# Norm and gate at the ends of two scan layers: from phases over the whole image to a pipeline of tiles, with the inverse deviation taken once per pixel

## The chip, the cores and the metric

The kernel runs on one core of a Trainium2 chip. The metric is the time of one execution in microseconds (us) of device time; smaller is better. PE is the matrix engine (TensorE), PEld its weight loads, DVE is VectorE, ACT is ScalarE, POOL is GpSimd, SP issues nearly all DMAs. Every engine takes its instructions in program order and waits on semaphores. SBUF is the on-chip memory, PSUM the eight banks into which PE writes; POOL has no work on PSUM in this kernel.

## The reference, cut to what matters

Four layers run one after the other on an image x of 4 x 96 x 56 x 56: attention (layer 0), a scan layer with eight directions (layer 1), a local-window layer (layer 2) and a scan layer with four directions and a convolution block (layer 3). The change touches only what follows the scans in layers 1 and 3:

```
# layer 1, after the scans: y has 192 channels per pixel
mu  = y.mean(-1);  var = mean((y - mu)**2)            # over the 192 channels of a pixel
y   = (y - mu) / sqrt(var + 1e-5) * ln_w + ln_b
y   = y * silu(z)                                      # the gate
out = einsum('bhwd,od->bohw', y, w_out)                # 192 -> 96, then added to x

# layer 3, after the scans
u = ((y - mu) / sqrt(var + 1e-5) * ln_g + ln_b) * z    # the same norm and gate
t = relu(bn1(conv1x1(u, 192 -> 384)))
t = relu(bn2(depthwise3x3(t)))
t = conv1x1(t, 384 -> 96)
s = sigmoid(se2(relu(se1(t.mean over pixels))))
out = t + t * s                                        # then added to x
```

## The kernel before

The program is a list of stages. `chip.stage(pe, act, dve, pool, sp)` gives each engine its own instruction list, and a stage ends for all engines together: the next one starts behind a barrier. The order inside a stage is written by hand, with semaphores between the engines; no planner is at work.

Images are handled in pairs: 64 partitions hold channels of image 0, the other 64 those of image 1, so the 192 channels are three groups c of 64, and `yacc` is [128, 3 x 56 x w] (w is the row width, 64 in layer 1 and 56 in layer 3). A pixel tile is 8 rows of 56, T = 448 columns, and there are NT = 7 tiles. Each scan layer does, for each of the two pairs, a front, the scans, and a tail. So there are four tails: two of layer 1 (`tail1`, L1470) and two of layer 3 (`tail3`, L1567).

`TailNorm` (L1372) works through the tiles t. PE multiplies the three groups of `yacc` by `blk`, a block matrix that averages over 64 channels, and adds them up in PSUM: the mean, already copied to all 64 partitions of the image (L1392). DVE subtracts it (L1426). ACT squares (L1411), PE averages the squares in the same way (L1400), ACT takes the root of 128 x 448 (L1418), DVE takes the reciprocal of 128 x 448 (L1431) into `rstd`. Each pixel's value stands there 64 times. DVE does tile t's subtraction before tile t-1's reciprocal.

`Gate` (L1434) starts after the last reciprocal. For each tile and group DVE does y * lg * rstd (L1450) and (y + lb) * z (L1454). z comes from DRAM, two tiles deep (L1461).

In `tail1` PE multiplies each gated tile by `wo` for image 0 and image 1 (L1492, three matmuls each) into two PSUM banks, and DVE adds x (L1509). DVE's list has all 14 additions behind the whole gate, so PE, after two results, waits for the end of the gate.

In `tail3` the norm and the gate are a stage of their own (`tail3_norm`, L1574), and the convolution block is the next one (`tail3_block`, L1616). The block loads its weights and then takes image i = 0, 1. The first convolution makes 3 groups x 7 tiles (L1659), which ACT drains into a padded image `pad` (L1698). Only when all 21 are drained does the depthwise convolution begin. DVE does groups 0 and 1 as nine multiply-adds per tile (`taps`, L738 and L741); PE does group 2 as nine matmuls with diagonal matrices (L1671). ACT applies bn2 and relu (L1708, L1713), PE does the third convolution (L1647), ACT keeps it in `t3` with a running sum (L1689). After seven tiles the small dense layers on the mean follow (L1679, L1681), and DVE writes the result (L1740). Then the next image starts.

Of the kernel before, what the change touches and what calls it, by code (L numbers as in the profile page):

```python
# [7 lines left out]
F32 = mybir.dt.float32  # L8
# [9 lines left out]
C = 96  # L18
# [1353 lines left out]
class TailNorm:  # L1372


    def __init__(self, chip, sb, sems, K, yacc, w):
        self.PS, self.K, self.yacc, self.w = chip.PS, K, yacc, w
        self.rstd = sb("rstd", [128, L])
        self.sq = sb("sq", [128, 2, 3, T])
        self.sd = sb("sd", [128, 2, T])
        self.mean, self.centred, self.squared = sems("mean"), sems("centred"), sems("squared")  # L1380
        self.var, self.std, self.inverse = sems("var"), sems("std"), sems("inverse")
# [4 lines left out]
    def pe(self, e):  # L1386
        for t in range(NT + 1):
            if t < NT:
                if t >= 2:
                    e.wait_ge(self.centred, t - 1)  # L1390
                for c in range(3):
                    a = e.matmul(self.PS[:, t % 2, 0:T], self.K["blk"][:], self.y(c, t), start=(c == 0), stop=(c == 2))  # L1392
                a.then_inc(self.mean, 1)
            if t:
                u = t - 1
                e.wait_ge(self.squared, t)
                if u >= 2:
                    e.wait_ge(self.inverse, u - 1)
                for c in range(3):
                    a = e.matmul(self.PS[:, 2 + u % 2, 0:T], self.K["blk"][:], self.sq[:, u % 2, c, :],  # L1400
                                 start=(c == 0), stop=(c == 2))
                a.then_inc(self.var, 1)

    def act(self, e):
        for t in range(NT + 1):
            if t < NT:
                e.wait_ge(self.centred, t + 1)
                if t >= 2:
                    e.wait_ge(self.var, t - 1)
                for c in range(3):  # L1410
                    a = e.activation(rows8(self.sq[:, t % 2, c, :]), self.y(c, t), ACT.Square)  # L1411
                a.then_inc(self.squared, 1)
            if t:
                u = t - 1
                e.wait_ge(self.var, t)
                if u >= 2:
                    e.wait_ge(self.inverse, u - 1)
                e.activation(self.sd[:, u % 2, :], self.PS[:, 2 + u % 2, 0:T], ACT.Sqrt,  # L1418
                             bias=self.K["eps5"][:]).then_inc(self.std, 1)

    def dve(self, e):
        for t in range(NT + 1):
            if t < NT:
                e.wait_ge(self.mean, t + 1)
                for c in range(3):
                    a = e.tensor_tensor(self.y(c, t), self.y(c, t), rows8(self.PS[:, t % 2, 0:T]), ALU.subtract)  # L1426
                a.then_inc(self.centred, 1)
            if t:
                u = t - 1
                e.wait_ge(self.std, t)  # L1430
                e.reciprocal(self.rstd[:, u * T:u * T + T], self.sd[:, u % 2, :]).then_inc(self.inverse, 1)  # L1431
# [1052 lines left out]
```

## Time and profile before

| | us |
|---|---|
| median of 3 runs (18067.99 to 18101.3) | 18072.52 |
| the profiled execution's own time | 18087.81 |
| its span, first to last instruction | 18086.0 |
| the two tails of layer 1, from their first DMA to the next stage's | 6348.3 to 6462.7; 10602.7 to 10719.3 |
| the two tails of layer 3 | 14489.9 to 14880.6; 17693.6 to the end |

The profile is one execution. A row of the timeline view has the start, the duration, the engine, the source line, what is written from what, the number of instructions merged in the row, and in brackets how long the engine was idle before it and who ended that. A row of the window view has, for one stretch, each engine's busy time and instruction count, then the TensorE clock granted (1.00 is 2.4 GHz, 0.50 is 1.2 GHz), the DMA share and GB/s. A matmul of fp32 data counts as two records.

### The profile page before, as it was taken

The page shows a single profiled execution, that of the slowest core. Times are in us where ns is not written, and L with a number is a line of the kernel's source. Part 1 is how long each engine was busy: PE and PEld are TensorE (multiplying, and loading weights), DVE is VectorE, ACT ScalarE, POOL GpSimd, SP SyncE. Part 2 cuts the span into 40 slices and gives each one's busy share as a digit, 9 for nine tenths or more (in the row PEclk, how much of TensorE's full clock was granted, in tenths as well). Part 3 has the DMA queues.
Part 4 walks back from the last instruction along what each step waited for, and adds up shares of the span by engine and source line. Part 5 has one row for each costly group of instructions (what it writes and reads, how often), then busy time and mean ns, then how long its engine had stood idle before and what let it go on. Part 6 is the DMA issues. An engine that isn't in the chain of part 4 may idle for free. (4 is left out here: it accounts for less than half of the span.)

```text
span 18086.0 us, 184332 instructions
## 1 busy us (share of the span) xinstructions
PE 14292.3 (79%) x38972; PEld 5918.2 (33%) x38972; DVE 15507.5 (86%) x20601; ACT 11827.0 (65%) x24107; POOL 12383.2 (68%) x5929
## 2 busy tenths in 40 slices
PE   7998878888888868888888868767777767777776
PEld 2222233333333323333333325423333233333333
DVE  6666489999999979999999964489999958999996
ACT  3555556667777636767677734378888827888882
POOL 0000079999999939999999941179988806998881
PEclk9999899999999989999999977788888888888888
DMA  1000033333333323333333321122222212222220
GB/s 27 13 18 11 12 93 107 106 107 107 107 107 106 102 77 106 108 106 107 107 106 107 106 78 37 37 67 81 82 79 79 78 29 72 81 81 79 79 80 29
DMA packets 542714, 1404.62 MB, mean 78 GB/s; under 512 B 135503, under 2 KB 191863, under 8 KB 538599
## 3 DMA queue, kind: packets, MB, share of 16 engines
q1 hardware_dynamic: 541586, 1392.84, 27.0%
q14 instruction: 817, 6.69, 0.1%
q8 instruction: 311, 5.10, 0.1%
HBM read 1311.24 MB, written 58.30 MB: 76 GB/s over the span
## 5 line engine op out<-in xcount | busy, mean ns | idle before, releaser
L996 PE MATMUL PS<-Hc,ident 128*128 128x448 f32 x16128 | 7494.1, 598 | 1950.8 <-POOL Hc L1308 1596.6
L1300 POOL TENSOR_TENSOR Tr<-du,BC 128x1344 f32<-128x1344 f32 x2688 | 8161.1, 3036 | 60.7 <-DVE du L1179 60.5
L996 PEld LDWEIGHTS PS<-Hc,ident 128*128 128x128 f32 x16128 | 3106.2, 205 | 6212.5 <-POOL Hc L1308 2579.3
L1118 ACT ACTIVATE PS<-dl,A 128x448 f32<-128x448 f32 x5376 | 3403.3, 633 | 2049.9 <-DVE Hr L1226 1248.6
L1308 POOL TENSOR_TENSOR Hc<-Hr,BC 128x448 f32<-128x448 f32 (+1 forms) x2688 | 3892.6, 1448 | 1030.1 <-DVE Hr L1226 947.2
L1226 DVE TENSOR_TENSOR_SCAN PS<-PS,st,Tr 128x448 f32<-128x448 f32 x3072 | 3358.2, 1135 | 142.8 <-ACT st L1132 140.6
L1233 DVE TENSOR_TENSOR Hc<-PS,BC 128x448 f32<-128x448 f32 x4480 | 2564.0, 605 | 0.0
L1126 ACT ACTIVATE PS<-cs,lneps,A 128x448 f32<-128x448 f32 x2688 | 1941.0, 722 | 175.2 <-DVE PS L1226 171.6
L719 POOL MEMSET pad<- 128x348 f32 x6 | 2.3, 387 | 2800.6 <-POOLq L67 2800.6
L1209 DVE SCALAR_TENSOR_TENSOR PS<-PS,Tr 128x448 f32<-128x448 f32 x2688 | 1644.2, 612 | 225.0 <-ACT PS L1126 214.0
L1118 ACT ACTIVATE Ar<-dl,A 128x448 f32<-128x448 f32 x2688 | 1765.5, 657 | 0.0
L1226 DVE TENSOR_TENSOR_SCAN Hr<-PS,st,Tr 128x448 f32<-128x448 f32 x1536 | 1749.9, 1139 | 0.0
L1226 DVE TENSOR_TENSOR_SCAN Hr<-Ar,st,PS 128x448 f32<-128x448 f32 x1536 | 1742.3, 1134 | 0.0
L521 DVE TENSOR_REDUCE mx<-PS 128x1 f32<-128x448 f32 (+1 forms) x2100 | 1207.7, 618 | 569.8 <-PE PS L311 554.4
L470 ACT ACTIVATE Pr<-PS 128x896 f32<-128x896 f32 (+1 forms) x1092 | 953.7, 887 | 675.6 <-PE PS L374 672.0
L1226 DVE TENSOR_TENSOR_SCAN PS<-Ar,st,PS 128x448 f32<-128x448 f32 x768 | 877.7, 1143 | 0.0
L311 PE MATMUL PS<-K,Q 96*128 96x448 bf16 (+1 forms) x2100 | 799.5, 388 | 89.2 <-DVE mx L521 56.0
L1132 ACT ACTIVATE st<-PS 128x2 f32<-128x2 f32 (+1 forms) x2688 | 448.8, 167 | 637.8 <-DVE Hc L1233 622.4
L958 PE MATMUL PS<-dts,dw 12*128 12x448 f32 x1008 | 540.2, 616 | 347.0 <-ACT dl L1054 320.1
L1007 PE MATMUL PS<-yacc,ident 128*128 128x448 f32 (+15 forms) x1320 | 761.5, 685 | 36.6 <-ACT yacc L1109 36.2
L374 PE MATMUL PS<-Q,K 99*128 99x448 bf16 (+1 forms) x2100 | 750.7, 371 | 6.2 <-ACT Q L439 3.6
L953 PE MATMUL PS<-xs,xp 128*76 128x448 f32 x1008 | 472.5, 611 | 292.2 <-ACT xs L1031 291.9
(254 smaller groups left out, 16125.1 us busy)
## 6 DMA issues: line engine op xcount, KB each, us to landing
BC<-bcscratch SPq DMA_DIRECT2D x5376, 224.0 KB, 3.6
zscratch<-zst SPq DMA_DIRECT2D x84, 224.0 KB, 2.0
bcscratch<-rows SPq DMA_DIRECT2D x336, 56.0 KB, 2.9
z<-zscratch SPq DMA_DIRECT2D x28, 672.0 KB, 4.5
xg<-mid SPq DMA_DIRECT2D x12, 1176.0 KB, 8.3
xr<-mid SPq DMA_DIRECT2D x56, 168.0 KB, 2.6
rl<-rows SPq DMA_DIRECT2D x56, 168.0 KB, 3.5
Q<-part SPq DMA_DIRECT2D x72, 98.0 KB, 4.4
```

The source lines that it names most:

```text
L311: e.matmul(PS[0:qn, 5 + n % 2, 0:T], Q[s][0:96, q0:q0 + qn], KK[s][0:96, i * T:i * T + T], start=True, stop=True).then_inc(mx_mm, 1)
L470: e.activation(Pr[0:kn, n % NPR, 0:nt, :], PS[0:kn, 2 * (n % 2):2 * (n % 2) + nt, 0:T], ACT.Exp, scale=scale).then_inc(s_exp, 1)
L521: e.tensor_reduce(mx[0:qn, t, i:i + 1], PS[0:qn, 5 + n % 2, 0:T], AX.X, ALU.max).then_inc(mx_red, 1)
L996: e.matmul(PS[:, YB + c, 0:T], K["ident"][:], Hc[:, g % NHC, c, :], start=False, stop=(nn == 15)).then_inc(y_done, 1)
L1007: e.matmul(view(PS[:, YB + c, :], ro, rd), K["ident"][:], view(yacc, c * n + off, dims), start=(i == 0), stop=False)
L1118: e.activation(decay_at(u), dl[:, q % 2, c, :], ACT.Exp, scale=A[:, q // NT, c, nn:nn + 1]).then_inc(a_done, 1)
L1126: e.activation(PS[:, u % NW, 0:T], cs[:, q % 2, c, :], ACT.Tanh, scale=A2[:, q // NT, c, nn:nn + 1], bias=K["lneps"][:]).then_inc(w_done, 1)
L1209: e.scalar_tensor_tensor(out=p, in0=p, scalar=1.0, in1=Tr[:, g % NTR, c, :], op0=ALU.add, op1=ALU.mult).then_inc(t2_done, 1)
L1226: e.tensor_tensor_scan(state_at(g, c), decay_at(u), PS[:, u % NW, 0:T] if ratio else Tr[:, g % NTR, c, :], 0.0 if q % NT == 0 else st[:, n ...
L1233: e.tensor_tensor(Hc[:, g % NHC, c, :], state_at(g, c), BC[:, g % NBS, 1, :], ALU.mult).then_inc(h_done, 1)
L1300: e.tensor_tensor(Tr[:, g % NTR], du[:, q % 2], b, ALU.mult).then_inc(t_done, 1)
L1308: e.tensor_tensor(Hc[:, g % NHC, ON_DVE:3], Hr[:, g % NH], c_, ALU.mult).then_inc(hp_done, 1)
```

## The change

1. `TailNorm` and `Gate` become one class, `NormGate`, whose steps are methods for one tile, and each engine's list goes by rounds r: tile r is centred and squared, tile r-1 is normalised and scaled, tile r-2 is shifted and gated, tile r-3 goes into the layer's next matmuls.
2. The mean: DVE adds the three groups (two additions), PE does one matmul instead of three.
3. The deviation: POOL adds the three squares (two additions); PE then multiplies with the sums as the stationary operand and two columns of `blk` as the moving one, so that pixels stand on partitions: 112 x 8 values per tile for both images. ACT's root and DVE's reciprocal are of 112 x 8. ACT copies them to 112 x 512 (`wide`), and four matmuls with the identity spread them to 128 x 448 in PSUM.
4. The scaling stays on DVE (L1474 of the new kernel), the shift by lb goes to ACT, the product with z to POOL.
5. In layer 1 the output matmuls use four PSUM banks and the additions of x stand in the rounds.
6. In layer 3 norm, gate and block are one stage, in rounds over 14 steps k (7 tiles x 2 images): the first convolution of step r-3, the depthwise one of step r-5, the third of step r-6. The depthwise group 2 is PE's only in the 8 steps of `PE_TAPS`; in the other 6 DVE does it too. `t3` holds both images, and the result is written and stored in halves.

```diff
+    def dve_sum(self, e, t):
+        s = rows8(self.ysum[:, t % 2, :])
+        ...
+        e.tensor_tensor(s, self.y(0, t), self.y(1, t), ALU.add).then_inc(self.summed, 1)
+        e.wait_ge(self.summed, 2 * t + 1)
+        e.tensor_tensor(s, s, self.y(2, t), ALU.add).then_inc(self.summed, 1)
+    def pe_mean(self, e, t):
+        e.wait_ge(self.summed, 2 * t + 2)
+        ...
+        e.matmul(self.PS[:, 5, 0:T], self.K["blk"][:], self.ysum[:, t % 2, :], start=True, stop=True).then_inc(self.mean_mm, 1)
+    def pool_sum(self, e, t):
+        s = self.sqsum[:, t % 2, :]
+        e.wait_ge(self.squared, t + 1)
+        ...
+        e.tensor_tensor(s, self.sq[:, t % 2, 0, :], self.sq[:, t % 2, 1, :], ALU.add).then_inc(self.sq_summed, 1)
+        e.wait_ge(self.sq_summed, 2 * t + 1)
+        e.tensor_tensor(s, s, self.sq[:, t % 2, 2, :], ALU.add).then_inc(self.sq_summed, 1)
+    def pe_var(self, e, t):
+        ...
+        for q in range(4):
+            a = e.matmul(self.PS[0:112, 6, 2 * q:2 * q + 2], self.sqsum[:, t % 2, 112 * q:112 * q + 112],
+                         self.K["blk"][:, 0:128:64], start=True, stop=True)
+    def act_root(self, e, t):
+        ...
+        e.activation(self.sd[:, t % 2, :], self.PS[0:112, 6, 0:8], ACT.Sqrt, bias=self.K["eps5"][0:112, :]).then_inc(self.rooted, 1)
-                e.reciprocal(self.rstd[:, u * T:u * T + T], self.sd[:, u % 2, :]).then_inc(self.inverse, 1)
+        e.reciprocal(self.rs[:, t % 2, :], self.sd[:, t % 2, :]).then_inc(self.inverse, 1)
+    def act_widen(self, e, t):
+        ...
+        e.activation(self.wide[:, t % 2].rearrange("p q (i c) -> p (q i) c", i=2),
+                     self.rs[:, t % 2, :].unsqueeze(2).broadcast_to([112, 8, 64]), ACT.Copy).then_inc(self.widened, 1)
+    def pe_spread(self, e, t):
+        e.wait_ge(self.widened, t + 1)
+        ...
+        for q in range(4):
+            a = e.matmul(self.PS[:, 7, 112 * q:112 * q + 112], self.wide[:, t % 2, q, :], self.K["ident"][0:112, 0:112],
+                         start=True, stop=True)
+    def dve_scale(self, e, t):
+        ...
+            a = e.scalar_tensor_tensor(out=y, in0=y, scalar=self.lg[:, c:c + 1], in1=rows8(self.PS[:, 7, 0:T]), op0=ALU.mult, op1=ALU.mult)
+    def act_shift(self, e, t):
+        ...
+            a = e.activation(self.y(c, t), self.y(c, t), ACT.Identity, bias=self.lb[:, c:c + 1])
+    def pool_gate(self, e, t):
+        e.wait_ge(self.shifted, t + 1)
+        e.wait_ge(self.z_ld[t % 2], 16 * (t // 2 + 1))
+        for c in range(3):
+            a = e.tensor_tensor(self.y(c, t), self.y(c, t), rows8(self.z[:, t % 2, c, :]), ALU.mult)
...
+PE_TAPS = (0, 1, 2, 4, 6, 8, 11, 13)
...
         def pe(e):
...
+            e.wait_ge(w_ld, 112)
+            for r in range(NK + 6):
+                if r < NT:
+                    norm.pe_mean(e, r)
+                if 0 <= r - 1 < NT:
+                    norm.pe_var(e, r - 1)
+                if 0 <= r - 3 < NK:
+                    expand(r - 3, 0)
+                if 0 <= r - 1 < NT:
+                    norm.pe_spread(e, r - 1)
+                if 0 <= r - 3 < NK:
+                    expand(r - 3, 1)
+                    expand(r - 3, 2)
+                if r - 5 in PE_TAPS:
+                    tap(r - 5)
...
+                if 0 <= r - 6 < NK:
+                    reduce_(r - 6)
```

DVE in layer 3, the first tail, from the gate into the block before (`rstd` inverse deviations, `w_484` the weights of the first convolution, `pad` its padded output, `acc` the depthwise sums):

```order
 L1450 SCALAR_TENSOR_TENSOR yacc<-yacc,lg,rstd 128x448
 L1454 SCALAR_TENSOR_TENSOR yacc<-yacc,lb,z 128x448
 L39 UNCONDITIONAL_BRANCH
 L42 UNCONDITIONAL_BRANCH
 L1724 MEMSET w_484 128x2304
 L738 TENSOR_SCALAR acc<-pad,cw 128x448
 L741 SCALAR_TENSOR_TENSOR acc<-pad,cw,acc 128x448 x8
```

The same place now, rounds 5 and 6 (`rs` inverse deviations by pixel):

```order
 L1410 TENSOR_TENSOR yacc<-yacc,PS 128x448 x3
 L1451 RECIPROCAL rs<-sd 112x8
 L738 TENSOR_SCALAR acc<-pad,cw 128x448
 L741 SCALAR_TENSOR_TENSOR acc<-pad,cw,acc 128x448 x8
 L1474 SCALAR_TENSOR_TENSOR yacc<-yacc,lg,PS 128x448 x3
 L738 TENSOR_SCALAR acc<-pad,cw 128x448
 L741 SCALAR_TENSOR_TENSOR acc<-pad,cw,acc 128x448 x8
 L1410 TENSOR_TENSOR yacc<-yacc,PS 128x448 x3
```

The depthwise sums of the first steps stand between the centring and the scaling of tiles 5 and 6, with no stage border in front.

PE in the first tail of layer 1, from the norm to the output matmuls before (`sq` squares, `wo` output weights):

```order
-L1392 MATMUL PS<-yacc,blk 128x448 x3
-L1400 MATMUL PS<-sq,blk 128x448 x6
-L1492 MATMUL PS<-yacc,wo 96x448 x42
```

And one round of it now (`ysum` sum of the groups, `sqsum` sum of the squares, `wide` the copied inverses):

```order
+L1405 MATMUL PS<-ysum,blk 128x448
+L1436 MATMUL PS<-blk,sqsum 112x2 x4
+L1525 MATMUL PS<-yacc,wo 96x448 x3
+L1465 MATMUL PS<-ident,wide 128x112 x4
+L1525 MATMUL PS<-yacc,wo 96x448 x3
```

The output matmuls of tile r-3 stand on both sides of the spread of tile r-1, and the mean of the next tile stands behind the second three.

## Rows read from the trace of the kernel before

**Rows 1.** The page: busy time, share of the span, instructions.
```profile
PE 14292.3 (79%) x38972; PEld 5918.2 (33%) x38972; DVE 15507.5 (86%) x20601; ACT 11827.0 (65%) x24107; POOL 12383.2 (68%) x5929
```
**Rows 2.** Windows: PE, PEld, DVE, ACT, POOL busy, clock, DMA; the tails by stage.
```profile
6348.30:6462.70 114.40, 72.77 (x168) 31.75 (x168) 67.70 (x85) 15.70 (x29) 0.01 (x1) 0.85 0.29 86
10602.70:10719.30 116.60, 72.88 (x168) 31.54 (x168) 67.70 (x85) 15.70 (x29) 0.00 (x0) 0.82 0.29 84
14489.90:14574.00 84.10, 37.88 (x84) 17.06 (x84) 60.02 (x80) 16.18 (x31) 0.00 (x0) 0.76 0.19 58
14574.00:14880.60 306.60, 244.27 (x596) 115.31 (x596) 173.34 (x259) 71.72 (x117) 16.56 (x30) 0.89 0.07 19
17693.60:17778.40 84.80, 39.02 (x84) 17.77 (x84) 60.03 (x80) 16.18 (x31) 0.01 (x1) 0.74 0.19 57
17778.40:18086.00 307.60, 244.82 (x596) 115.17 (x596) 173.33 (x259) 71.70 (x117) 16.55 (x29) 0.89 0.07 19
```
**Rows 3.** Timeline, first tail of layer 1, the norm.
```profile
6352.47 1.68 DVE L1426 TENSOR_TENSOR yacc<-yacc,PS 128x448 f32<-128x448 f32 x3 [3.43 <-PE PS L1392]
...
6371.02 1.51 ACT L1411 ACTIVATE sq<-yacc 128x448 f32<-128x448 f32 x3 [4.55 <-DVE yacc L1426]
6372.44 0.61 ACT L1418 ACTIVATE sd<-PS,eps 128x448 f32<-128x448 f32 x1
6372.58 2.52 PE L1400 MATMUL PS<-sq,blk 128*128 128x448 f32 x6 [1.80 <-ACT sq L1411]
6373.08 2.95 DVE L1431 RECIPROCAL rstd<-sd 128x448 f32<-128x448 f32 x1 [2.09 <-ACT sd L1418]
```
**Rows 4.** Timeline, the same tail, gate and output.
```profile
6400.31 0.68 DVE L1450 SCALAR_TENSOR_TENSOR yacc<-yacc,lg,rstd 128x448 f32<-128x448 f32 x1
...
6436.55 0.62 DVE L1509 TENSOR_TENSOR yo<-PS,xr 96x448 f32<-96x448 f32 x1 [1.63 <-PE PS L1492]
...
6459.10 0.62 DVE L1509 TENSOR_TENSOR yo<-PS,xr 96x448 f32<-96x448 f32 x1 [1.63 <-PE PS L1492]
```
**Rows 5.** Groups by form: count, busy us, mean ns, idle before.
```profile
L1431 DVE RECIPROCAL rstd<-sd 128x448 f32<-128x448 f32 x28 | 82.7, 2952 | 62.5 <-ACT sd L1418 62.5
L1308 POOL TENSOR_TENSOR Hc<-Hr,BC 128x448 f32<-128x448 f32 x1792 | 2026.7, 1131 | 507.1 <-DVE Hr L1226 436.9
L1698 ACT ACTIVATE pad<-PS,bn1o 128x448 f32<-128x448 f32 x84 | 61.0, 726 | 222.2 <-PE PS L1659 222.2
```
**Rows 6.** Timeline, a 112 x 112 fp32 matmul of layer 2, six of them.
```profile
10909.86 1.44 PE L1929 MATMUL PS<-dg,E 112*84 112x112 f32 x12
```
**Rows 7.** Timeline, layer 3's block: weights' arrival, DVE's waits, one group.
```profile
14582.19 18.13 PE L1659 MATMUL PS<-yacc,w 128*128 128x448 f32 x40 [42.15 <-DMA w<-in_c1w]
...
14633.51 0.45 DVE L738 TENSOR_SCALAR acc<-pad,cw 128x448 f32<-128x448 f32 x1 [56.93 <-ACT pad L1698]
...
14639.65 0.45 DVE L738 TENSOR_SCALAR acc<-pad,cw 128x448 f32<-128x448 f32 x1
...
14776.79 0.45 DVE L738 TENSOR_SCALAR acc<-pad,cw 128x448 f32<-128x448 f32 x1 [45.16 <-ACT pad L1698]
```
**Rows 8.** Timeline, end of the program: last depthwise sum to store.
```profile
18061.97 5.73 DVE L741 SCALAR_TENSOR_TENSOR acc<-pad,cw,acc 128x448 f32<-128x448 f32 x8
...
18079.14 0.32 SPq L1758 DMA_DIRECT2D out<-xr  x1
```
**Rows 9.** PE's third convolution after waits of two lengths.
```profile
17900.65 2.50 PE L1647 MATMUL PS<-cv,w 128*96 128x448 f32 x6 [1.30 <-ACT cv L1713]
...
17912.91 3.97 PE L1647 MATMUL PS<-cv,w 128*96 128x448 f32 x6 [3.00 <-ACT cv L1713]
```
**Rows 10.** DVE and POOL together, in a front.
```profile
2290.34 5.90 DVE L741 SCALAR_TENSOR_TENSOR acc<-pad,cw,acc 128x448 f32<-128x448 f32 x8
2290.74 0.71 POOL L851 COPY xc<-xc 128x448 f32<-128x448 f32 x1 [65.09 <-ACT xc L819]
```

**Rows 11.** The page: DMA issues, KB each, us to landing.
```profile
z<-zscratch SPq DMA_DIRECT2D x28, 672.0 KB, 4.5
```

More of the change, by code:

```diff
@@ L1404, in act @@
[L1404 to L1419, printed above, removed]
@@ L1477, in tail1 @@
         wo_zero, w_ld, l_ld = sems("wo_zero"), sems("w_ld"), sems("l_ld")
-        norm = TailNorm(chip, sb, sems, K, yacc, w)
-        gate = Gate(sb, sems, norm, zd, pair, lg, lb)
+        norm = NormGate(chip, sb, sems, K, yacc, w, zd, pair, lg, lb)
         out_mm, added = sems("out_mm"), sems("added")
@@ new lines, in pe, with drain, relu @@
+            squeeze(1)
+            excite(1)
+        def act(e):
+            def drain(k, c):
+                t = k % NT
+                u = place[k, c]
+                if u == 0:
+                    e.wait_ge(pad_zero, 1)
+                    e.wait_ge(folds[0].step, 5)
+                if k >= NT:
+                    e.wait_ge(tapped, 9 * tap_groups(min(k - NT + 1, NT - 1)))
+                    e.wait_ge(relued, min(k - NT + 2, NT))
+                e.wait_ge(full, u + 1)
+                e.activation(pad[:, c, 1 + 8 * t:9 + 8 * t, 1:57], rows8(PS[:, u % 4, 0:T]), ACT.Relu,
+                             scale=bn1[:, 0, c:c + 1], bias=bn1[:, 1, c:c + 1]).then_inc(drained, 1)
+            def relu(k):
+                v = k % 2
+                if k == 0:
+                    e.wait_ge(folds[1].step, 5)
+                if k >= 2:
+                    e.wait_ge(red_mm, k - 1)
+                if k in PE_TAPS:
+                    u = place[k, "tap"]
@@ new lines, in act @@
+            e.wait_ge(l_ld, 96)
+            for f in folds:
+                f.act(e)
+            e.wait_ge(w_ld, 112)
+            for r in range(NK + 7):
+                if 0 <= r - 2 < NT:
+                    norm.act_shift(e, r - 2)
+                if r < NT:
+                    norm.act_square(e, r)
+                if 0 <= r - 1 < NT:
+                    norm.act_root(e, r - 1)
+                    norm.act_widen(e, r - 1)
+                if r == NT + 8:
+                    squeeze(0)
+                if 0 <= r - 7 < NK:
+                    keep(r - 7)
+                if 0 <= r - 6 < NK:
+                    relu(r - 6)
+                if r == NT + 8:
+                    excite(0)
+                for c in range(3):
+                    if 0 <= r - 3 < NK:
+                        drain(r - 3, c)
@@ L1748, in sp @@
         def sp(e):
+            for t, k in ((lg, "l3lg"), (lb, "l3lb"), (b1, "c1b"), (b2, "c2b"), (folds[0].t, "bn1"), (folds[1].t, "bn2")):
+                e.dma_start(t[:], D[k]).then_inc(l_ld, 16)
+            for t in range(2):
+                norm.load(e, t)
             for t, k in ((cw, "c2w"), (w3, "c3w"), (c3b, "c3b"), (s1w, "s1w"), (s1b, "s1b"), (s2w, "s2w"), (s2b, "s2b")):
```

476 lines of the change are left out of this document (261 added, 215 removed).

## The prediction

> **What bounds the kernel now.** I read the page first: DVE is busy 86% of the span, PE 79% [rows 1]. That average is set by the scans, where the change does nothing, so the next view is the windows over the four tails. They last 114.4, 116.6, 84.1 + 306.6 and 84.8 + 307.6 us, 1014.1 in all, 5.6% of the span. DVE is busy 602 us of that, PE 712, POOL 33 [rows 2]: nobody is full, the engines take turns. The timeline says how. In the norm one tile takes 6.58 us, a closed loop: reciprocal 2.95, the next subtraction 1.61, squares 1.51, root 0.61, reciprocal again [rows 3]. The gate is DVE's alone, 84 instructions at two per 1.4 us, about 29 us per tail. In layer 1 PE then makes the outputs, one per 2.25 us [rows 4]. In the block DVE stands still 56.9 and 45.2 us while PE makes the first convolution of an image, then works without a gap at 6.13 us per group of nine [rows 7].
>
> **Durations of the new steps.** Known from rows: three subtractions 1.65, three squares 1.51, three matmuls 2.25 (0.75 each) with 0.2 more until the last is done [rows 3, 4]. Two additions of SBUF tiles on DVE: like the subtraction, 0.55 each, 1.25 with the wait between them. Scaling: three of 0.68, less their overlap, 1.9 [rows 4]. Shift on ACT: like the squares, 1.6. POOL: 1.13 per product or sum [rows 5], so 2.3 for the two sums and 3.4 for the gate. Copy to 112 x 512: a square of 448 is 0.5, so 0.65. The trace does not show the small steps. A root of 112 x 8 lies between 0.1 and the 0.61 of the large one, a reciprocal of 8 between 8/448 of 2.95, that is 0.05, and 0.6 of any DVE instruction; I take 0.25 for each, nearer to the lower ends because work by element is gone. Four small matmuls: the nearest row is six of 112 x 112 in 1.44, 0.24 each [rows 6], so 1.0 and 1.2 until done; upper end 0.4 each, if weight loads of 128 columns don't hide. Hand-over between engines: 0.05 (square ends 6372.53, PE starts 6372.58) [rows 3].
>
> The Trainium skill weighs against item 3 here: "GPSIMD Engine Reference", section "Key points", says that POOL shares its SBUF interfaces with VectorE and that instructions with two SBUF inputs contend. The trace agrees in size: eight multiply-adds of DVE took 5.90 beside one 0.71 us copy of POOL [rows 10], and 5.73 alone [rows 8].
> From these rows alone: 0.17 us per 0.71 of POOL, so 0.3 per POOL instruction of 1.13. About 12 of them per layer-3 tail fall beside depthwise sums, 4 us; in layer 1 the pairs of additions meet some, 2 us.
>
> **Tail of layer 1.** Fill: the first subtraction ends 5.8 us after the start as now [rows 3]. Then tile 0: squares 1.5, sums 2.3, small matmuls 1.2, root and reciprocal 0.5 (with the table load that stands there now too, and ACT still squaring tile 1, some 2.5 more), copy 0.65, spread 1.2, scale 1.9, shift 1.6: 19 us. POOL must sum tile 2 first, whose squares are behind the shift: 1.5 + 2.3; gate 3.4. The first output matmul starts at about 29.
> Then the rounds. The loop in one is: subtraction 1.65, squares 1.5, root 0.25, reciprocal 0.25, copy 0.65, spread 1.2, three output matmuls 2.25 that stand in front of the next mean, mean 0.95, eight hand-overs 0.4: 9.1, with a small lag 9.3. DVE's own work is 7 per round, POOL's 5.7, PE's 7.2, so the loop binds. Three rounds bring outputs 0 to 5: 57. The next has no mean: 8.3, so 65.5. Six outputs are left, 13.5 plus 2 for the last gate: 81. Addition 0.6, store and barrier 3.0 (6459.72 to 6462.7 now [rows 4]): 85. With 2 for contention 87. Gains 27.4 and 29.6, together 57.
>
> **Tail of layer 3.** DVE's work grows: 34 groups instead of 28, since 6 of 14 steps keep all three, 34 x 6.13 = 208.4. What goes is the standing still.
> Start: PE waits for seven small loads that now stand behind six others and two z loads in SP's queue: 15 issues of about half a us and a landing. Now the block needs 8.2 us from its start to its weights [rows 7], the new stage about 11 to 13. The wait holds the first mean, so everything. Rounds 1 to 4 then run as in layer 1, with PE's 6.75 of first convolution (3 x 2.25) in rounds 3 and 4: first depthwise group at about 64. Rounds 5 and 6 are PE's: small norm work with its ends 3.1, first convolution 6.75, depthwise on PE 9 x 0.75 = 6.75, third 2.25, 19 together, against 12.3 of groups and 5 of norm on DVE. So at about 99 four groups are done. From there DVE has no wait: 30 x 6.13 = 183.9, last scaling 1.9, image 0's result 3.9: 289. PE needs 6.75 to 15.75 per round there, against 12.3 and 18.4 of DVE, and by the two-step lead it stays ahead. ACT's drains, 0.73 each [rows 5], lie beside that. From the last group to the last store 11.4 as now (18067.7 to 18079.14) [rows 8]: 300. The store now takes 6.9 to the end of the span [rows 2, 8]; half the size, 4.5. Sum 304.5, with 4 for contention 308. Gains 390.7 - 308 = 82.7 and 392.4 - 308 = 84.4: 167.
>
> **Sum.** 57 + 167 = 224. Against the profiled execution 18087.8 that makes 17864; against the median of the runs, 15.3 lower, 17849. I forecast 17849. The scans, fronts and the other layers have the same instructions. Lower end: no contention (12 less) and small steps at the low ends (8 rounds x 0.5 x 4, 16 less): 17821. Upper end of the same mechanism: small matmuls at 0.4 instead of 0.24 put 1.3 on each of the 8 rounds' loops twice over: 10 per tail, 42 in all: 17891.
>
> **Rivals.**
> A: PE paces the block. If reductions, drains and depthwise matmuls wait for each other within a round (bank u waits for the drain of u-4, which waits behind ACT's relu, which waits for DVE), the rounds with PE groups cost PE's 15.75 and not the mean of PE and DVE: 8 x 3.5 = 28 more per tail, 56 in all, or as much from a slow clock in half of them. For it: the first convolution of step k+2 and DVE's groups of step k hang on the same ACT queue. Against: in rounds 5 to 18 DVE has some 222 of work, PE 173 (81 + 54 + 29 + 9). Time 17905.
> B: z arrives late. SP issues z of tile t+2 behind stores that wait for additions. A load lands 4.5 us after its issue [rows 11]. If POOL waits for a whole landing in 5 rounds of both layer-1 tails, that is 45 us: 17894. Layer 3 has no stores in between. The lead of about one round, 9 us, speaks against it.
> C: slower than before. PE's clock: after a wait of 1.30 us six records took 2.50, after 3.00 us 3.97 [rows 9], near 1.2 GHz. The new rounds have waits inside them in place of one long one between phases. If PE ran at 1.2 GHz through all four tails, it would need in a layer-3 tail 247 large matmuls x 1.5 + 56 small x 0.5 = 398, plus fill and end 52: 450; a layer-1 tail, with spread, output and mean doubled in the loop, 125. Sum 1150 against 1014: 136 slower, 18209. DVE's 254 (208 of groups, 7 x 5.1 of norm, some 10 of the rest) hides PE's 199 (247 x 0.75 + 56 x 0.24) up to a factor of 1.3; the gain is gone at about 1.7 (199 x 1.7 + 52 is the 390 of now), a mean clock of 0.6. Against: the tails are at 0.74 to 0.89 now, with waits [rows 2].
> The Trainium skill has the rule for this: "TensorE: Matmul & The Clock Gate", section "HAM oscillation", tells of a kernel that waits between its bursts and starts every burst slow. By rows 9 that holds for waits of 3 us; the rounds' longest is about that in the fill only.
> D: better than the forecast, because the fill (64 us in layer 3) is shorter and contention nil: 17810.
>
> **How the numbers follow.** Forecast 0.62; A 0.20; B 0.07; C 0.04; D 0.05; 0.02 that it gains nothing for a reason not seen. The range 17815 to 17930 leaves out D's far end, C and the worst of A: about 0.15. The measurement tells apart 0.2%, 36 us. Faster by more than that: all of forecast, A, B and D, less a little, 0.94; within 0.02; slower 0.04.
>
> **What would show it.** Right: no 128 x 448 reciprocal, and reciprocals of 112 x 8 near 0.2; rounds of 9 to 9.5 us in layer 1; the block's DVE from the fourth group on without idle time until image 1 ends; DVE's waits of 56.9 and 45.2 us gone, in their place waits of a few us between the norm's steps until the first group; stages of 87 and 308. Wrong: DVE idle before its groups behind ACT (A), POOL idle behind the z load (B), a granted clock under 0.65 in the tails (C), multiply-adds of DVE well over 0.69 in more than a few places. The whole would be wrong if the other stages change their length by more than 10 us.

## The result, and the profile after

The changed kernel took 17862.85 us in the median of four runs (17858.43 to 17872.52), the kernel before 18080.18 beside it (median of four runs, the three behind the 18072.52 above among them): ratio 0.9879, 95% interval 0.9862 to 0.9896. A second set of runs on another occasion gave 17867.53 and 0.9884 (0.9871 to 0.9898). The forecast was 17849.

The page first: busy time, share, instructions, as in [rows 1].

```profile
span 17859.1 us, 184766 instructions
PE 14124.2 (79%) x38924; PEld 5866.3 (33%) x38924; DVE 15511.5 (87%) x20685; ACT 11881.7 (67%) x24219; POOL 12534.2 (70%) x6033
```

Over the whole span DVE is as busy as before (15507.5 then), and the span is 226.9 us shorter. That total hides two opposite moves, which the windows below show against [rows 2]: in a layer-1 tail DVE's busy time fell from 67.7 to 44.1 and 44.6 us, since half of the gate and nearly all of the reciprocal left it, and in a layer-3 tail it rose from 233.4 to 259.0 and 259.6, since it took six more groups. In layer 3 the gain is therefore waiting that went. In layer 1 the tails lost 30 us each, and DVE's work shrank by 23 to 24 at the same time; no run changed the order and left the work where it was, so the two are not told apart there. The windows over the four tails, columns as in [rows 2]; in layer 3 one window stands where there were two:

```profile
6341.50:6425.80 84.30, 62.11 (x210) 34.16 (x210) 44.11 (x78) 29.94 (x57) 39.34 (x35) 0.78 0.39 117
10562.90:10648.90 86.00, 61.24 (x210) 33.47 (x210) 44.64 (x78) 29.93 (x57) 40.08 (x35) 0.81 0.38 114
14417.50:14731.90 314.40, 222.95 (x614) 111.78 (x614) 259.04 (x388) 99.27 (x176) 50.30 (x46) 0.85 0.12 34
17546.00:17859.10 313.10, 224.29 (x614) 112.45 (x614) 259.61 (x388) 99.47 (x176) 50.68 (x46) 0.84 0.12 34
```

The tails last 797.8 us against 1014.1: 216.3 less, where 224 was forecast. Layer 1 gave 60.7 (57 forecast), layer 3 155.6 (167 forecast). The other 10.6 of the span's difference lie outside the tails (18086.0 - 1014.1 = 17071.9 before, 17061.3 after). The eleven executions of the experiments have 17039.6 to 17075.9 there, with the same instructions in all of them, so this is scatter, and the windows of the tails measure the change better than the whole time does.

One round of layer 1 in the timeline (start, length, engine and line; in brackets the idle time before and what ended it), to hold against the loop of [rows 3]:

```profile
6379.19 1.67 DVE L1410 TENSOR_TENSOR yacc<-yacc,PS 128x448 f32<-128x448 f32 x3
6380.89 1.51 ACT L1418 ACTIVATE sq<-yacc 128x448 f32<-128x448 f32 x3 [2.34 <-DVE yacc L1410]
6382.30 0.25 ACT L1444 ACTIVATE sd<-PS,eps 112x8 f32<-112x8 f32 x1
6382.58 0.20 DVE L1451 RECIPROCAL rs<-sd 112x8 f32<-112x8 f32 x1 [1.73 <-ACT sd L1444]
6382.82 0.63 ACT L1457 ACTIVATE wide<-rs 112x512 f32<-112x512 f32 x1 [0.27 <-DVE rs L1451]
6383.50 1.81 PE L1465 MATMUL PS<-ident,wide 112*128 112x112 f32 x8 [2.17 <-ACT wide L1457]
...
6385.35 1.86 DVE L1474 SCALAR_TENSOR_TENSOR yacc<-yacc,lg,PS 128x448 f32<-128x448 f32 x3 [2.06 <-PE PS L1465]
...
6389.36 1.15 DVE L1410 TENSOR_TENSOR yacc<-yacc,PS 128x448 f32<-128x448 f32 x2
```

From subtraction to subtraction 10.17 us. The reciprocal's 2.95 us have become 0.20, and from its start to the scale's it is 2.77 us still: widening and spreading stand there now.

The same view of VectorE in the first layer-3 tail: the weights' wait, the first groups, the last group and the end.

```profile
14428.77 0.63 DVE L1397 TENSOR_TENSOR ysum<-yacc 128x448 f32<-128x448 f32 x1 [4.90 <-DMA s2b<-in_s2b]
...
14481.97 0.20 DVE L1451 RECIPROCAL rs<-sd 112x8 f32<-112x8 f32 x1 [1.73 <-ACT sd L1444]
14482.09 1.15 DVE L738 TENSOR_SCALAR acc<-pad,cw 128x448 f32<-128x448 f32 x1
14483.27 8.74 DVE L741 SCALAR_TENSOR_TENSOR acc<-pad,cw,acc 128x448 f32<-128x448 f32 x8
...
14494.18 5.73 DVE L741 SCALAR_TENSOR_TENSOR acc<-pad,cw,acc 128x448 f32<-128x448 f32 x8
...
14504.54 8.75 DVE L741 SCALAR_TENSOR_TENSOR acc<-pad,cw,acc 128x448 f32<-128x448 f32 x8
...
14515.46 7.99 DVE L741 SCALAR_TENSOR_TENSOR acc<-pad,cw,acc 128x448 f32<-128x448 f32 x8
...
14523.48 0.40 DVE L738 TENSOR_SCALAR acc<-pad,cw 128x448 f32<-128x448 f32 x1
...
14531.82 7.98 DVE L741 SCALAR_TENSOR_TENSOR acc<-pad,cw,acc 128x448 f32<-128x448 f32 x8
...
14709.46 5.73 DVE L741 SCALAR_TENSOR_TENSOR acc<-pad,cw,acc 128x448 f32<-128x448 f32 x8
14720.85 0.16 DVE L1842 TENSOR_REDUCE sm<-sums 96x1 f32<-96x7 f32 x1 [5.67 <-ACT t L1795]
```

The waits of 56.9 and 45.2 us of [rows 7] are gone. From the fourth group's end (14523.4) to the last group's (14715.2) VectorE has no idle time. Groups of eight multiply-adds take 5.73 us, as in [rows 8], but four take 7.98 to 8.75. GpSimd in that stretch:

```profile
14481.86 1.12 POOL L1426 TENSOR_TENSOR sqsum<-sq 128x448 f32<-128x448 f32 x1 [4.79 <-ACT sq L1418]
14483.07 1.16 POOL L1428 TENSOR_TENSOR sqsum<-sqsum,sq 128x448 f32<-128x448 f32 x1
14484.19 4.46 POOL L1488 TENSOR_TENSOR yacc<-yacc,z 128x448 f32<-128x448 f32 x3
...
14516.96 4.57 POOL L1488 TENSOR_TENSOR yacc<-yacc,z 128x448 f32<-128x448 f32 x3 [7.04 <-ACT yacc L1481]
14533.32 4.56 POOL L1488 TENSOR_TENSOR yacc<-yacc,z 128x448 f32<-128x448 f32 x3 [11.79 <-ACT yacc L1481]
```

Each long group lies beside a row of three products like these (the one beside the group of 14504.54 starts at 14505.46 and takes 4.46), and these rows are long too: in layer 1, where VectorE is idle or reads PSUM meanwhile, three products take 3.32 us.

### The profile page after: what moved, and what is told of

It reads as the page before. It is cut to its first block and busy times, and to the rows that moved or that the text cites. A ratio compares the mean times of both kernels' runs of the same rounds, so it can differ in the third digit from the quotient of the medians.

```text
span 17859.1 us, 184766 instructions
## 1 busy us (share of the span) xinstructions
PE 14124.2 (79%) x38924; PEld 5866.3 (33%) x38924; DVE 15511.5 (87%) x20685; ACT 11881.7 (67%) x24219; POOL 12534.2 (70%) x6033
## 5 line engine op out<-in xcount | busy, mean ns | idle before, releaser
L1233 DVE TENSOR_TENSOR Hc<-PS,BC 128x448 f32<-128x448 f32 x4480 | 2563.5, 604 | 0.0
L741 DVE SCALAR_TENSOR_TENSOR acc<-pad,cw,acc 128x448 f32<-128x448 f32 x992 | 701.1, 707 | 35.5
```

The source lines that it names most:

```text
L741: e.scalar_tensor_tensor(out=o, in0=x, scalar=cw[:, c, k:k + 1], in1=o, op0=ALU.mult, op1=ALU.add).then_inc(done, 1)
L1233: e.tensor_tensor(Hc[:, g % NHC, c, :], state_at(g, c), BC[:, g % NBS, 1, :], ALU.mult).then_inc(h_done, 1)
```

## The experiments

For each kernel the four tails are read from its trace, from the tail's first load of its parameters to the next stage's first load (or the end of the span); "median" and ratio are of its runs against the kernel before in the same session. The rows marked * are one execution each.

| kernel | layer 1 | layer 3 | sum | median us | ratio |
|---|---|---|---|---|---|
| changed | 84.3, 86.0 | 314.4, 313.1 | 797.8 | 17862.85 | 0.9879 |
| only_tail1 | 84.4, 86.4 | 389.6, 388.9 | 949.3 | 18002.82 | 0.9961 |
| full_recip | 100.8, 103.1 | 323.1, 321.6 | 848.6 | 17903.49 | 0.9904 |
| recip_psum * | 93.0, 92.8 | 316.8, 318.0 | 820.6 | 17881.15 | |
| small_gate | 85.4, 86.9 | 305.4, 310.7 | 788.4 | 17844.74 | 0.9871 |
| dve_gate * | 86.7, 84.7 | 313.5, 312.8 | 797.7 | 17847.54 | |
| late_wait | 84.7, 84.5 | 310.5, 311.5 | 791.2 | 17842.92 | 0.9873 |
| taps11 | 86.5, 86.2 | 295.3, 297.5 | 765.5 | 17818.80 | 0.9863 |
| taps14 * | 84.2, 84.7 | 304.6, 304.8 | 778.3 | 17856.17 | |
| late_taps12 * | 86.8, 85.9 | 288.1, 288.4 | 749.2 | 17790.90 | |
| changed, again | 86.3, 85.9 | 313.6, 314.4 | 800.2 | 17867.53 | 0.9884 |
| final | 84.3, 86.4 | 287.3, 287.2 | 745.2 | 17803.68 | 0.9851 |

Intervals of the ratios are 0.0013 to 0.0017 to either side. A layer-1 tail that two kernels share differs by up to 2.6 us, and the layer-3 tail that only_tail1 shares with the kernel before by up to 3.5, so a difference of 1 to 3 us in one tail is not evidence by itself.

**Half the change: only_tail1.** `tail1` and `NormGate` as changed; `tail3`'s norm, gate and block stages as before.

> The first layer's tails as changed, the second layer's norm stage and convolution stage as before. If the gain is what each stage's own window shows, the two layer-1 tails take 84 and 86 us (114.4 and 116.6 before), the layer-3 stages stay at 84 + 307 us each, and the time is about 61 us below before: ratio 0.9966, some 18019 us. The rival is that part of the layer-3 gain, or of the 10 us that the changed kernel is shorter by outside its tails, comes from elsewhere in the program (the scan of layer 1, which starts earlier or later beside other transfers): then layer 3 of this kernel is shorter too, and the time is below 18010 us.

Measured: 84.4 and 86.4 us in layer 1, 389.6 and 388.9 in layer 3, 0.9961 (0.9946 to 0.9976). The gain is local, stage by stage. The median, 18002.8, was 16 us under the expectation, which alone would have pointed to the rival; the windows show layer 3 shorter by 1 to 3.5 us only and the rest (17049.2 us) inside its scatter.

**The reciprocal of 128x448 back: full_recip.**

```diff
-        for q in range(4):
-            a = e.matmul(self.PS[0:112, 6, 2 * q:2 * q + 2], self.sqsum[:, t % 2, 112 * q:112 * q + 112], ...)
+        a = e.matmul(self.PS[:, 6, 0:T], self.K["blk"][:], self.sqsum[:, t % 2, :], start=True, stop=True)
...
-            a = e.scalar_tensor_tensor(out=y, ..., in1=rows8(self.PS[:, 7, 0:T]), ...)
+            a = e.scalar_tensor_tensor(out=y, ..., in1=rows8(self.rs[:, t % 2, :]), ...)
```

Root and reciprocal are of 128x448 here, and the widening and the spread are left out.

> The pipeline and the one stage of layer 3 are kept, but the variance goes through one 128x448 product with the averaging matrix, and root and reciprocal are taken of 128x448, with no widening and no spreading products. Theory: what a round waits for is a chain, and the chain from the small reciprocal (0.20) over the widening (0.63) and the spreading products to the scale's start is already 2.8 to 3.0 us, as long as a reciprocal of 128x448 alone (2.95 in the kernel before). So the layer-1 tails grow only by the root (0.25 to about 0.5 us a round, 8 rounds): 86 and 88 us. In layer 3 VectorE sets the pace from the first depthwise group on, and three reciprocals lie behind it, 3 x 2.75 = 8 us, with 2 us before it: 324 us a tail. Sum about 24 us above the changed kernel, 17887 us, ratio 0.9892. The rival: the small reciprocal is where the gain comes from, as VectorE's busy time has it: 28 x 2.75 = 77 us more, 17940 us, ratio 0.992.

Measured: 50.8 us more in the tails (848.6 - 797.8), between the two theories (24 and 77). Layer 3 came near the expected 10 (8.7 and 8.5 us more), by luck in part, as the next run shows; layer 1 did not: 16.5 and 17.1 more in place of 2. VectorE's groups of that tail (count, busy us, mean ns, idle before), first with the large reciprocal, then of the changed kernel:

```profile
L1471 DVE SCALAR_TENSOR_TENSOR yacc<-yacc,lg,rs 128x448 f32<-128x448 f32 x21 | 20.9, 1045 | 0.1
L1448 DVE RECIPROCAL rs<-sd 128x448 f32<-128x448 f32 x7 | 20.7, 2953 | 15.8 <-ACT sd L1441 15.8
```

```profile
L1474 DVE SCALAR_TENSOR_TENSOR yacc<-yacc,lg,PS 128x448 f32<-128x448 f32 x21 | 13.0, 676 | 14.6 <-PE PS L1465 14.6
L1451 DVE RECIPROCAL rs<-sd 112x8 f32<-112x8 f32 x7 | 1.4, 203 | 13.3 <-ACT sd L1444 13.3
```

The scale, the same arithmetic on the same shape, went from 676 to 1045 ns, 7.9 us a tail. What had changed in this instruction is where its second operand lies: SBUF in place of PSUM.

**The operand moved: recip_psum.** Against full_recip:

```diff
-        e.reciprocal(self.rs[:, t % 2, :], self.sd[:, t % 2, :])
+        e.reciprocal(self.PS[:, 7, 0:T], self.sd[:, t % 2, :])
```

The scale reads the same bank. One bank stands in place of two buffers, so the reciprocal also waits for the scale of the tile before, which stands ahead of it in VectorE's list in any case.

> As the kernel with the reciprocal of 128x448, but VectorE writes the reciprocal into a PSUM bank and the scale reads it there, not in SBUF. In that kernel the scale's 21 instructions took 20.9 us of a layer-1 tail, the longest 1552 ns, against 13.0 us and 672 to 681 ns where they read PSUM. Theory: an instruction of VectorE with both tensors in SBUF is stretched while GpSimd's product runs, one with a tensor in PSUM is not. So the scale goes back to 675 ns and 13.0 us, and the layer-1 tails shrink by nearly 8 us each, 93 and 95 us; in layer 3 (20.0 us now) by 5 to 7 us of the 323 and 322. The rival: the scale is slower because GpSimd's product or the matmuls read the same tensor y at that time; then it stays near 1 us an instruction and the tails keep 101 and 103 us.

Measured: 93.0, 92.8, 316.8 and 318.0 us. One line of code, all its instructions in the trace (least, median and longest ns), with the operand in SBUF and in PSUM:

```profile
L1471 DVE SCALAR_TENSOR_TENSOR yacc<-yacc,lg,rs x84: 671/682/1552, 6344.5 to 17710.8; 128x448 f32<-128x448 f32 x84
```

```profile
L1471 DVE SCALAR_TENSOR_TENSOR yacc<-yacc,lg,PS x84: 664/676/681, 6346.8 to 17676.8; 128x448 f32<-128x448 f32 x84
```

The operand in PSUM takes 848.6 - 820.6 = 28 us off the tails. The rival, that GpSimd's product or the matmuls read the same `yacc` at that time, is refuted: they still do. So 28 of full_recip's 51 us are contention that came with the operand in SBUF, and the narrow root and reciprocal with all that belongs to them are worth the other 820.6 - 797.8 = 23, of one execution and so known to a few us. By VectorE's busy time it would have been 77.

The chain had given 24, but in other places, so that the agreement is luck: it put 2 us on a layer-1 tail and 10 on a layer-3 tail, and the differences are 8.7 and 6.8 in layer 1 and 2.4 and 4.9 in layer 3. In the first layer-1 tail GpSimd's waits for z behind the last rounds are 4.84 and 3.96 us here, against 1.16 and 2.82 in the changed kernel: late z, the prediction's rival B, is part of the 8.7. In layer 3 GpSimd's two sums of squares and the start of its product now fall beside the reciprocal and no longer beside a group: two groups take 7.23 us in place of 8.75, and their first products 0.38 in place of 1.15, so 4.6 us of contention go as the long reciprocals come.

**GpSimd's product cut: small_gate.** In layer 3, tiles 3 to 6, `y, z = y[:, 0:1, :], z[:, 0:1, :]` ahead of the product, so that 56 of 448 columns are gated and the others are left out.

> In layer 3 POOL's product with z for tiles 3 to 6 covers only the first 56 of 448 columns; the other columns of these tiles are left without the gate. All else as changed. Theory: the four depthwise groups that VectorE runs beside these products are longer for that: 8.74, 8.75, 7.99 and 7.98 against 5.73 us, of which the product has 2.26 us each (7.99 - 5.73, the groups that no sum of squares lies beside). They come down to 6.5, 6.5, 5.7 and 5.7 us, and each layer-3 tail is 9 us shorter: 305 and 304 us, 18 us in all. The rival: these groups are longer for another reason (their place behind a wait, the matmuls' reads, ScalarE's), they keep 8 to 8.7 us, and the tails stay at 314 us.

VectorE in the second of the loaded rounds, against 8.75 and 7.99 above:

```profile
14503.20 6.49 DVE L741 SCALAR_TENSOR_TENSOR acc<-pad,cw,acc 128x448 f32<-128x448 f32 x8
...
14511.86 5.73 DVE L741 SCALAR_TENSOR_TENSOR acc<-pad,cw,acc 128x448 f32<-128x448 f32 x8
14518.54 0.20 DVE L1451 RECIPROCAL rs<-sd 112x8 f32<-112x8 f32 x1 [0.95 <-ACT sd L1444]
```

The mechanism and its size are shown: 2.26 us a group, 9 us in the first layer-3 tail. The first of these groups keeps 0.76 us over 5.73; the second sum of squares still runs beside its start. The second tail gained 2.4 us only, not 9: its first group came 1.6 us later than in the changed kernel (64.4 us into the stage, not 62.8), and the reciprocal of tile 6 was waited for.

```profile
17620.29 6.92 PE L1708 MATMUL PS<-yacc,w 128*128 128x448 f32 x12
...
17627.06 6.93 PE L1719 MATMUL PS<-pad,diag 128*128 128x448 f32 x18
...
17637.27 0.20 DVE L1451 RECIPROCAL rs<-sd 112x8 f32<-112x8 f32 x1 [4.03 <-ACT sd L1444]
```

The same twelve records took 4.69 us in the first tail. There the granted clock was 1.00 (14502.8 to 14508.3); here it was 0.50 (17618.4 to 17624.0). So TensorE came 2.2 us later to its 18 depthwise records, the variance products stand behind these, and VectorE's next group stands behind the reciprocal. When VectorE's groups shrink, TensorE's order is the next thing late.

**The same product on VectorE: dve_gate.** Tiles 3 to 6 in layer 3: `e.scalar_tensor_tensor(out=y, in0=y, scalar=lb, in1=z, op0=ALU.add, op1=ALU.mult)`, without ScalarE's shift.

> In layer 3 the gate of tiles 3 to 6 goes from ScalarE (shift) and GpSimd (product) to VectorE, as (y + beta) * z in one instruction for each channel block, in the round in which GpSimd had it. Theory: the product beside a group costs VectorE 2.26 us (7.99 against 5.73 us); four of them, 9.0 us a tail. On VectorE itself a tile costs 3 instructions of 0.62 us as the scale does (1.86 us), 7.4 us for four. So the two nearly cancel: the tails are 313 and 312 us, 1 to 2 us shorter. The rival: it is the engine that counts and not the neighbour, all that VectorE gets is added: 314 + 7 = 321 us. A second rival is that the reciprocal of tile 6 is then waited for (it was, by 0.95 and 4.03 us, where the product had been cut), and half of what is won goes there.

Measured: 313.5 and 312.8 us. All its groups take 5.73 us again, and the gates took what that won:

```profile
14494.69 3.45 DVE L1497 SCALAR_TENSOR_TENSOR yacc<-yacc,lb,z 128x448 f32<-128x448 f32 x3
...
14498.54 5.73 DVE L741 SCALAR_TENSOR_TENSOR acc<-pad,cw,acc 128x448 f32<-128x448 f32 x8
...
14513.93 1.86 DVE L1497 SCALAR_TENSOR_TENSOR yacc<-yacc,lb,z 128x448 f32<-128x448 f32 x3
```

Of the four gates two took 3.45 us, those beside the sums of squares, and two 1.86: 10.6 us, not 7.4. The reciprocal of tile 6 was waited for by 1.63 us besides. Giving GpSimd the product costs VectorE 2.26 us a tile, and doing it itself costs 1.86 or more: in this place the offload is worth nothing.

**The weights' wait: late_wait.**

```diff
-            e.wait_ge(w_ld, 112)            # ahead of all rounds, on PE, ACT and DVE
             for r in range(NK + 5):
+                if r == 5:                  # DVE; PE r == 6, ACT r == 7, POOL r == 2
+                    e.wait_ge(w_ld, 112)
```

> In the one stage of layer 3, the wait for the seven weights' transfers is taken at the weights' first use (VectorE and GpSimd in the rounds before the first depthwise group, TensorE and ScalarE behind it) and not ahead of the norm. Theory: VectorE waits there 4.9 us for the last of them, 11.2 us from the stage's start, and all that follows up to the first depthwise group is a chain, so the first group starts about 4 us earlier (60.5 us from the start, not 64.5) and each layer-3 tail is 4 us shorter: 310 and 309 us. The rival: the wait only moves; z of the first tiles, the affine weights or the first 1x1 weights (which stand behind the seven transfers in the same queue) or the zeroing of the padded buffer come last in its place, and less than 1 us is left.

```profile
14405.98 0.63 DVE L1397 TENSOR_TENSOR ysum<-yacc 128x448 f32<-128x448 f32 x1 [1.27 <-PEq L67]
...
14466.09 1.15 DVE L738 TENSOR_SCALAR acc<-pad,cw 128x448 f32<-128x448 f32 x1
```

The first depthwise instruction starts 60.2 us into the stage (64.6 in the changed kernel), in the second tail 60.3 (62.8). The tails are 3.9 and 1.6 us shorter, where the theory had 4. The 1.6 is within the scatter; what shows the effect in the second tail is its first group, 2.5 us earlier.

**The balance of the two engines: taps11, taps14.** `PE_TAPS` with 11 and with 14 tiles in place of 8.

> As changed, but TensorE takes the third channel block's depthwise products of 11 tiles of 14 (0, 1, 2, 3, 4, 5, 7, 8, 10, 11, 13) and not of 8: VectorE has 31 groups left of 34. Theory: VectorE alone sets the pace of the block in the changed kernel too (no idle time between the fourth group and the last), so each group less is worth 6.13 us: 3 x 6.13 = 18.4 us a layer-3 tail, 296 and 295 us, less what TensorE's longer rounds give back (18 records of 6.93 us for each such tile; 2 to 4 us where two of them follow each other): 297 to 300 us, some 30 to 35 us below the changed kernel in all. The rival: TensorE already paces part of the block (rival A of the prediction), and the tails stay at 310 us or above.

> As changed, but TensorE takes the third channel block of all 14 tiles; VectorE has 28 groups, six fewer. If VectorE were the only bound, the layer-3 tails would come to 314 - 6 x 6.13 = 277 us. Theory: TensorE becomes it. A tile costs it 6.93 (expansion) + 6.93 (depthwise) + 2.42 (reduction) = 16.3 us at the full clock, 14 of them 228 us, with the norm's products (7 x about 4.5) and a first expansion that starts some 33 us into the stage, and 15 us behind the last reduction: 305 to 310 us, no more than 10 us below the changed kernel's 314, and above the tails with 11 tiles.

Measured: 295.3 and 297.5 us with 11, 304.6 and 304.8 with 14. Three groups less on VectorE (18.4 us by 6.13) gave 19.1 and 15.6: with 8 tiles VectorE alone paces the block. With 14, VectorE's waits in the first tail (total, times, longest) have a new head:

```profile
DVE acc L738 <- ACT pad L1771: 25.3, 5, 15.2
DVE rs L1451 <- ACT sd L1444: 11.0, 6, 2.4
```

The groups wait 25.3 us for ScalarE's drains (L1771), which stand behind TensorE's expansions. So the best number lies between 8 and 14.

**Both: late_taps12, and timed again as final.**

> The late wait for the weights and 12 tiles of 14 with the third channel block on TensorE (all but 7 and 10). Theory: the two are independent. Four groups less are 4 x 6.13 = 24.5 us a tail, the late wait 4 and 2 us as measured alone; TensorE has 12 x 16.3 + 2 x 9.35 = 214 us of the block against VectorE's 30 x 6.13 = 184 us, so it now waits for TensorE in places: 288 to 295 us a tail. The rival: TensorE is the bound already at 12 tiles, and this is no shorter than 11 tiles would be with the late wait (293 us), or longer.

> The changed kernel itself once more, for comparison on the same chip: 17863 us within 10, its tails 84, 86, 314 and 313 us within 2. Its tails are the same from one execution to the next to 1 or 2 us, while the rest of the program (the front ends and scans, 17039 to 17076 us in the kernels run so far, none of which touches it) scatters by more.

> The late wait and 12 tiles with the third channel block on TensorE, timed: tails of 86, 86, 288 and 288 us as in its first execution, 797.6 - 748 = 49 us below the changed kernel's; with the rest of the program its own scatter, 17800 to 17820 us, ratio 0.985 to 0.986. The rival: the 17791 us of the one execution were a stroke of luck in the rest, and the layer-3 tails' gain is given back elsewhere: 17840 us or more.

Late_taps12's tails were 288.1 and 288.4 us, final's (the same kernel) 287.3 and 287.2. That is 25 to 27 us under the changed kernel's tails, where four groups (24.5) and the late wait's 3.9 and 1.6 make 28.4 and 26.1: within 3 us the two edits add up. 12 tiles without the late wait were not tried, nor 13. Final's windows of layer 3, columns as in [rows 2]:

```profile
14414.50:14701.80 287.30, 241.00 (x686) 124.17 (x686) 233.50 (x352) 98.45 (x176) 50.26 (x46) 0.90 0.13 37
17514.50:17801.70 287.20, 240.86 (x686) 124.43 (x686) 233.53 (x352) 98.46 (x176) 50.28 (x46) 0.89 0.13 37
```

TensorE and VectorE are now about equally busy, at 241 and 234 of 287 us. Final took 17803.68 us (17796.06 to 17818.02), 0.9851 (0.9837 to 0.9864) of before, against 0.9884 for the changed kernel in the same session: 0.36% faster than it (17803.68 against 17867.53), and the fastest version here. The 17791 of the one execution was low by its rest (17039.6 against 17056.5).

## Why the prediction was right, and where it was off

- **The bound, "the engines take turns".** Right as far as the windows show it: all four tails together keep DVE busy for 607 us, against 602 before, and lost 216 us. only_tail1 shows 60 of it to be layer 1's own. How much of that is overlap, and how much the work that left DVE, is open.
- **The small steps, 0.25 us each for root and reciprocal of 112 x 8.** Measured 0.25 and 0.20 (medians of 28).
- **Layer 1: first output matmul at 29 us, rounds of 9.3, tail 87.** Measured 26.9, 9.8, 10.2 and 8.5 (starts of L1410 at 6369.36, 6379.19, 6389.36, 6397.89), 84.3 and 86.0. The loop was the right thing to sum. The 29 was not what its own terms make: 19, 1.5 + 2.3 and 3.4 are 26.2, close to what came, and the surplus of nearly 3 us is about what the first tail came out under 87. The sign "rounds of 9 to 9.5" held for the mean only. The round of 10.2 is one in which TensorE was slow: granted clock 0.66 (6383.5 to 6388.5), against 1.00 in the round of 8.5 (6393.7 to 6397.0).
- **Layer 3: weights at 11 to 13, first group at 64, four groups done at 99, last group at 289.** Measured 11.2, 64.6, 105.9, 297.6. The order of events is right and nearly all of the excess arises between the first group and the sixth.
- **The step that was off: contention, "about 12 of them per layer-3 tail, 4 us".** It is 11.9 us in the first tail: the four groups are longer by 3.01, 3.02, 2.26 and 2.25 us, and two first products by 0.70 each (1.15 against 0.45). The count was near (four gates and two pairs of sums, 16 instructions); the price was not: 0.75 us for each of a gate's three instructions (2.26 / 3), where the estimate had 0.3. It came from [rows 10], a copy of 0.71 us, which reads one tensor; GpSimd's products read two. The prediction's "the trace agrees in size" has nothing to agree with, since the page that it cites states no size. And its own sign of being wrong, multiply-adds well over 0.69 us in more than a few places, came true in four of 34 groups a tail. 8 us more on 308 makes 316, and 314.4 and 313.1 were measured: all other terms together were 2 to 3 us too high.

  A better price stood in the trace before, overlooked. An instruction of VectorE with two SBUF tensors took 0.95 us beside a product of GpSimd (11422.02 to 11423.15), and 0.47 without one:

```profile
11422.54 0.95 DVE L2162 SCALAR_TENSOR_TENSOR E<-R,E 112x315 f32<-112x315 f32 x1
...
11442.66 0.47 DVE L2162 SCALAR_TENSOR_TENSOR E<-R,E 112x315 f32<-112x315 f32 x1
```

  One with a single SBUF tensor took 0.86 us where GpSimd was idle, and 2.81 beside a product of 3.03 us (12086.14 to 12089.17):

```profile
11840.85 0.86 DVE L1186 TENSOR_SCALAR w<-du 128x1344 f32<-128x1344 f32 x1 [10.30 <-ACT du L1059]
...
12087.07 2.81 DVE L1186 TENSOR_SCALAR w<-du 128x1344 f32<-128x1344 f32 x1
```

  The first says 0.48 us for an overlap of 0.6, the second 1.95 for an overlap of 2.1: two to three times the 0.3 that the prediction took for 1.13 us of GpSimd. The scans' instructions with one operand in PSUM, beside GpSimd nearly all the time, keep their length (L1233: 586 to 615 ns in 4480 of them). Both halves of what full_recip and recip_psum then showed could have been read from these rows.
- **A misreading without effect.** The gate before is 42 instructions a tail, not the 84 of the prediction (84 is one line's count over four tails); its 29 us are right.
- **Rival A, TensorE paces the block.** Refuted for 8 tiles by the gapless DVE and by taps11; it is what happens at 14. It was the right danger at another setting.
- **Rival B, z late.** Present in small, in the last two tiles of the first tail, inside its 84 us:

```profile
6407.97 3.32 POOL L1488 TENSOR_TENSOR yacc<-yacc,z 128x448 f32<-128x448 f32 x3 [1.16 <-DMA z<-zscratch]
6414.11 3.31 POOL L1488 TENSOR_TENSOR yacc<-yacc,z 128x448 f32<-128x448 f32 x3 [2.82 <-DMA z<-zscratch]
```

- **Rival C, TensorE's clock.** Refuted: the granted clock is 0.78 to 0.85 in the tails, and low for single stretches only. The first row here stands at 0.60 (14589.7 to 14593.6), after a wait of 2.36 us; a row of the same six records in 2.50 us, after a wait of 0.76, at 1.00 (14571.3 to 14573.6):

```profile
14589.69 4.05 PE L1725 MATMUL PS<-cv,w 128*96 128x448 f32 x6 [2.36 <-ACT cv L1788]
...
14601.94 2.50 PE L1725 MATMUL PS<-cv,w 128*96 128x448 f32 x6 [1.44 <-ACT cv L1788]
```

  The Trainium skill, "TensorE: Matmul & The Clock Gate", section "HAM oscillation", tells of a kernel that waits between its bursts and starts every burst slow; this trace shows that in places only.
- **Rival D, a shorter fill in layer 3 and no contention.** Neither came: the first group stood at 64.6 and 62.8, and contention was three times the forecast.
- **Left open.** In the rounds with groups VectorE still waits 1.73 us for the root ahead of the reciprocal; another place for it in VectorE's order was not tried. That the second layer-3 tail has its first group 1.8 us earlier than the first one comes from TensorE's clock: the spread and the twelve records behind it took 2.00 and 5.54 us in the first tail, 1.15 and 4.69 in the second (granted clock 0.55 and 1.00 over their first 3.8 us), 1.7 us in all.
- **The sum.** 224 forecast and 216 measured in the tails; 17849 lay 14 us under the median. The tails are 8 of that, and the base 7.7: the forecast was set against 18072.52, and the four runs beside the changed kernel gave 18080.18. (The 2 too many are inside the scatter.) The errors partly cancelled: layer 1's fill was put too long, layer 3's contention too low. And by its last sign, other stages changing by more than 10 us, the prediction would have been wrong (10.6 us); the sign was no good, for these stages scatter by 36 us with the same instructions.

## What to carry to other kernels

Sum the chain of a round, not an engine's busy time: a reciprocal that was 2.95 us on the busiest engine was worth 23 us over 28 tiles and not 77, because other steps took its place in the loop. The other 193 us came from overlap, fusion and the new division of work together; in layer 3 they are waits that went, in layer 1 the parts were not separated. Check such a chain by stage too, for its total can be right by luck. When work is shifted to GpSimd, price each of its instructions that will run beside VectorE's from a row of such a pair, and look at where VectorE's tensors lie: two in SBUF were costly here, one operand in PSUM was not. After a fusion set the split between engines anew: the table of taps was worth 23 to 24 us a layer-3 tail (310.5 to 287.3, 311.5 to 287.2).

## What the runs showed of the hardware

- The contention is mutual and large. The instructions of VectorE with both tensors in SBUF go from 0.7 to as much as 1.55 us beside GpSimd's two-input products (full_recip), and three of these products from 3.32 to between 4.46 and 4.57 us; with one operand in PSUM the same scale stays at 0.66 to 0.68 (recip_psum). The Trainium skill, "GPSIMD Engine Reference", section "Key points", names contention with VectorE instructions that have two SBUF inputs, without a size; the trace agrees with it and gives the size. Of instructions with one SBUF input it names only those in a "2-port perf mode". Here `TENSOR_SCALAR` with one SBUF input took 1.15 us in place of 0.45 beside GpSimd's sum, while full_recip's reciprocal, with one SBUF input too, stayed at 2.95 us in all 28 cases; whether the one runs in that mode and the other not, no run here tells.
- Three of GpSimd's products of 128x56 took 2.13 us (beside VectorE), three of 128x448 3.32 (beside none with two SBUF tensors): by these spans, which the profile gives roughly, much of an instruction does not depend on its length.
- The stages that no kernel touched scatter by 36 us between executions, ten times what a tail does (up to 3.5). Under 0.2% the windows decide here, not the median.
